# Linear attention with gapless context loads, and key sums from four GpSimd additions and one product

## The chip, the cores and the metric

The kernel is one launch on one core of a Trainium2 chip. The time is the device time of that launch in microseconds; the span of a profile is the time from the first to the last instruction of one profiled execution. Engines are named as in the profile: PE is TensorE (PEld its weight loads), DVE is VectorE, ACT is ScalarE, POOL is GpSimd, SP is SyncE, which here only issues DMAs.

## What is computed

Four attention layers follow each other on `x` (32 batch items of 56 tokens, 128 channels), each with the same context of 32 x 1500 x 128, all float32. Only the first layer is touched. For each item:

```python
Q_phi = elu(query)                      # 56 x 128
K_phi = elu(key)                        # 1500 x 128, key = value = context
KV = einsum('bnd,bne->bde', K_phi, value)
Z = 1.0 / (einsum('bnd,bd->bn', Q_phi, K_phi.sum(axis=1)) + 1e-6)
attn = einsum('bnd,bde->bne', Q_phi, KV) * Z[..., None]
x = query + attn                        # then a LayerNorm
```

`K_phi.sum(axis=1)` is the key sum: 128 numbers per item.

## The kernel before

`build` runs one stage after another, each in a block of its own that ends with all engines together. `load_phase` loads and transposes `x`; `linear_attention` is the stage of the change; then come the LayerNorms and projections, self attention, cross attention, full attention and the quantised layer. `linear_attention` also writes the transposed context of each item to DRAM (`ctx_turned`), which later stages read.

One item is a context matrix of 1500 rows. Row number 12 p + j lies on partition p (of KP = 125), slot j (of NJ = 12), so a partition holds 12 rows that are neighbours in DRAM, 6144 B. The tile `cn` has a 129th column in each slot that holds ones, set once per buffer by POOL (L264). There are four `cn` buffers. The loop over 32 items (`sweep`) writes out its first four steps, then loops, then drains. In step n the engines do:

- SP (L241 to L253) waits until item n-4 has been transposed, its product `kvp` is done (`kv_done`) and its `phi` is ready, and loads item n in two DMAs, of 112 and of 13 partitions (`CN_PARTS`). Each row of 128 floats is a piece of its own, because in the tile the next row begins 129 floats on. After the first four items SP issues 28 weight transfers (L257).
- DVE clips the item at zero (L311, `neg`), ACT takes the exponential (L354), and DVE makes `phi` = max(exp - 1, x) of the item before (L332).
- PE transposes the 12 slots of item n (L283), ACT copies them in three pieces to `ct` (L359, `turned_copied`), and POOL issues the store of `ct` to DRAM (L268).
- PE multiplies `phi` of item n-2 with `cn` of item n-2, all 129 columns, summed over the 12 slots (L292, `kvp`). Columns 0 to 127 are KV, column 128 is the key sum, thanks to the ones. DVE copies both to SBUF (L339, and L340, which spreads the sum over 128 columns).
- PE multiplies both with the queries of item n-3 (L300), ACT adds the epsilon (L350), DVE inverts and multiplies (L322, L324).

Each engine works strictly in its written order; semaphores named in the code join them. float32 products take two passes of weights and matmul each.

Of the kernel before, what the change touches and what calls it, by code (L numbers as in the profile page):

```python
# [5 lines left out]
ALU = mybir.AluOpType  # L6
# [6 lines left out]
B, NQ, NK, D = 32, 56, 1500, 128  # L13
# [204 lines left out]
def linear_attention(nc, m, w, ctx_in, ctx_turned):  # L218


    with ExitStack() as ctx:
        sb, ps, sem = memory(nc, ctx, "l0_")
        cn = [sb(f"cn{r}", [KP, NJ, D + 1]) for r in range(4)]
        neg = [sb(f"neg{p}", [KP, NJ, D]) for p in range(2)]
        phi = [sb(f"phi{p}", [KP, NJ, D]) for p in range(2)]
        ct = [sb(f"ct{p}", [128, NK]) for p in range(2)]
        kv = [sb(f"kv{p}", [128, 2, D]) for p in range(2)]
        den = [sb(f"den{p}", [128, NQ]) for p in range(2)]
# [4 lines left out]
        ctx_loaded = [sem(f"ctx_loaded{r}") for r in range(4)]  # L233
        ctx_stored = [sem(f"ctx_stored{p}") for p in range(2)]
        weights_loaded, loads = sem("weights_loaded"), weight_loads(m, w)[:EARLY]
        names = ("ones_set", "clipped", "exped", "phi_ready", "turned", "turned_copied",
                 "kv_done", "kv_copied", "ratio_done", "den_shifted", "den_inverted", "ratio_copied")
        (ones_set, clipped, exped, phi_ready, turned, turned_copied,
         kv_done, kv_copied, ratio_done, den_shifted, den_inverted, ratio_copied) = (sem(s) for s in names)

        with nc.Block() as block:  # L241
            @block.sync
            def _(sp):
                def step(n, r, live):
                    if live(4):
                        sp.wait_ge(turned, 3 * (n - 3))
                        sp.wait_ge(kv_done, n - 3)
                        sp.wait_ge(phi_ready, n - 3)
                    else:
                        sp.wait_ge(ones_set, 4)  # L250
                    rows = ctx_in[bass.ds(n, 1)].rearrange("o (p j) d -> (o p) j d", j=NJ)
                    for a, b in CN_PARTS:
                        sp.dma_start(cn[r][a:b, :, 0:D], rows[a:b]).then_inc(ctx_loaded[r], 16)  # L253

                def load_weights():
                    for dst, src in loads:
                        sp.dma_start(dst, src).then_inc(weights_loaded, 16)  # L257
                sweep(sp, step, 0, buffers=4, aside=load_weights)
                sp.wait_ge(weights_loaded, 16 * len(loads))

            @block.gpsimd
            def _(pool):
                for r in range(4):
                    pool.memset(cn[r][:, :, D:D + 1], 1.0).then_inc(ones_set, 1)  # L264

                def step(n, p, live):
                    pool.wait_ge(turned_copied, 3 * n + 3)
                    pool.dma_start(ctx_turned[bass.ds(n, 1)].rearrange("o d k -> (o d) k"), ct[p][:, :]  # L268
                                   ).then_inc(ctx_stored[p], 16)
                sweep(pool, step, 0)  # L270
                for p in range(2):
                    pool.wait_ge(ctx_stored[p], 16 * PAIRS)

            @block.tensor
            def _(pe):
                def step(n, r, live):
                    p = r % 2
                    if live(0):
                        pe.wait_ge(ctx_loaded[r], transfers(n, r, len(CN_PARTS), 4))
                        for j in range(NJ):  # L280
                            if j % 4 == 0 and live(1):
                                pe.wait_ge(turned_copied, 3 * n - 2 + j // 4)
                            last = pe.transpose(tp[:, j // 4, KP * (j % 4):KP * (j % 4) + KP], cn[r][:, j, 0:D],  # L283
                                                m.ident[0:KP, 0:KP])
                            if j % 4 == 3:
                                last.then_inc(turned, 1)
                    if live(2):
# [1 line left out]
                        if live(4):  # L289
                            pe.wait_ge(kv_copied, 2 * n - 6)  # L290
                        for j in range(NJ):
                            last = pe.matmul(kvp[:, p, 0:D + 1], phi[p][:, j, :], cn[(r - 2) % 4][:, j, :],  # L292
                                             start=j == 0, stop=j == NJ - 1)
                        last.then_inc(kv_done, 1)
                    if live(3):
                        pe.wait_ge(kv_copied, 2 * n - 4)
                        if live(4):
# [8 lines left out]
            def _(dve):  # L306
                def clip(n, r, live):
                    dve.wait_ge(ctx_loaded[r], transfers(n, r, len(CN_PARTS), 4))
                    if live(2):
                        dve.wait_ge(phi_ready, n - 1)  # L310
                    dve.tensor_scalar(neg[r % 2][:, :, :], cn[r][:, :, 0:D], 0.0, None, ALU.min  # L311
                                      ).then_inc(clipped, 1)

                def step(n, r, live):
# [11 lines left out]
                    if live(1):  # L326
                        q = (r - 1) % 4
                        dve.wait_ge(exped, n)
                        if live(3):
                            dve.wait_ge(kv_done, n - 2)  # L330

                        dve.scalar_tensor_tensor(out=phi[q % 2][:, :, :], in0=neg[q % 2][:, :, :], scalar=-1.0,  # L332
                                                 in1=cn[q][:, :, 0:D], op0=ALU.add, op1=ALU.max
                                                 ).then_inc(phi_ready, 1)
                    if live(2):
                        dve.wait_ge(kv_done, n - 1)
# [1604 lines left out]
```

## Time and profile before

| | |
|---|---|
| Median of 3 runs | 2575.98 us (2573.08 to 2579.17) |
| The profiled execution | 2577.91 us |
| Its span | 2576.4 us |
| PE busy | 2203.3 us (86%) |
| DVE busy | 1802.3 us (70%) |
| ACT busy | 1416.5 us (55%) |
| POOL busy | 708.9 us (28%) |
| HBM read, written | 127.01 MB, 25.49 MB |

The page also cuts the span into 40 slices of 64 us. The stage of the change lies in slices 1 to 4, where the DMA engines are busy for 7 to 9 tenths; they are idle in the slices after it. Shares over the whole span say little about one stage, so the stage is read by windows, waits and timelines of its own.

### The profile page before, as it was taken

To read this page: it belongs to the slowest core of one execution; us is meant where nothing else is said; L and a number is where in the kernel's file an instruction comes from. 1 tells how busy PE (TensorE), PEld (TensorE's weight loads), DVE (VectorE), ACT (ScalarE), POOL (GpSimd) and SP (SyncE) were. 2 spreads that over 40 slices of the span, in tenths; PEclk is the share of its full clock that TensorE was granted. 3 is DMA by queue.
4 is the path that set the end of the run, shared out by engine and by line. 5 is a ranking of instruction groups with operands and counts; after the bars stand their busy time and mean duration, and the time that the engine had idled before them with its cause. 6 is when DMAs were issued, how large, how long until landed. Compare 5 with 4: busy or idle time off the path is not lost. (4 is left out here: it accounts for less than half of the span.)

```text
span 2576.4 us, 60397 instructions
## 1 busy us (share of the span) xinstructions
PE 2203.3 (86%) x20341; PEld 1461.8 (57%) x20341; DVE 1802.3 (70%) x3608; ACT 1416.5 (55%) x2639; POOL 708.9 (28%) x538
## 2 busy tenths in 40 slices
PE   4777799869999999999987999544698888888888
PEld 4777477526666666666644767222365555555553
DVE  3555454567777777777734565799499999999984
ACT  2444232236666666666633444322398888888862
POOL 0000122111111111111000000232276666666640
PEclk7998655579999999999988999755699999999989
DMA  7896000013333223332206775000011111111100
GB/s 185 226 238 178 2 0 0 0 49 84 90 89 85 79 74 89 89 89 79 58 1 169 225 223 147 1 0 0 36 49 37 36 36 36 36 36 47 37 1 15
DMA packets 107834, 190.20 MB, mean 74 GB/s; under 512 B 19550, under 2 KB 74846, under 8 KB 107774
## 3 DMA queue, kind: packets, MB, share of 16 engines
q1 hardware_dynamic: 98558, 140.26, 19.8%
q0 software_dynamic: 9216, 49.16, 6.9%
q8 instruction: 36, 0.59, 0.1%
q14 instruction: 24, 0.20, 0.0%
HBM read 127.01 MB, written 25.49 MB: 59 GB/s over the span
## 5 line engine op out<-in xcount | busy, mean ns | idle before, releaser
L1025 DVE TENSOR_REDUCE c_part<-c_mxp 128x1 f32<-128x500 f32 x672 | 429.4, 674 | 172.7 <-PE c_mxp L914 168.4
L1634 ACT ACTIVATE c_e<-c_sp,alpha 128x750 f32<-128x750 f32 x448 | 392.8, 882 | 23.6 <-PE c_sp L1578 21.5
L998 ACT ACTIVATE c_e<-c_stp 125x896 f32<-125x896 f32 x384 | 351.9, 917 | 97.3 <-PE c_stp L926 96.8
L1592 PE MATMUL c_tp<-ident_h,c_ph 128*128 128x128 f16 x2688 | 230.6, 223 | 72.7 <-DVE c_pt L1654 70.8
L1592 PEld LDWEIGHTS c_tp<-ident_h,c_ph 128*128 128x128 f16 x2688 | 181.2, 100 | 167.6 <-DVE c_pt L1654 113.3
L914 PE MATMUL c_mxp<-c_kh,c_qb 128*128 128x500 f16 x672 | 254.4, 380 | 3.1 <-DVE c_part L1025 2.2
L1654 DVE TENSOR_SCALAR c_pt<-c_tp 125x768 bf16<-125x768 f16 x448 | 246.2, 550 | 3.4 <-PE c_tp L1592 1.9
L1548 POOL TENSOR_SCALAR c_ki<-c_clipped 128x500 bf16<-128x500 bf16 x96 | 191.8, 1998 | 151.6 <-DVE c_clipped L1665 139.5
L941 PE MATMUL c_pvp<-c_e,c_vx 125*32 125x168 f32 (+1 forms) x6144 | 226.9, 265 | 0.6 <-ACT c_e L998 0.4
L1698 DVE TENSOR_SCALAR c_ph<-c_e,c_inv 128x1500 f16<-128x1500 f32 x224 | 224.1, 1000 | 4.3
L941 PEld LDWEIGHTS c_pvp<-c_e,c_vx 125*32 125x32 f32 x6144 | 160.3, 109 | 117.1 <-issue 90.2
L868 POOL TENSOR_TENSOR c_qs<-qst,mask_quad_ 96x224 f16<-96x224 f32 (+1 forms) x128 | 67.5, 556 | 577.2 <-PE c_stp L926 577.2
L1578 PE MATMUL c_sp<-c_ki,c_qb 128*128 128x375 bf16 x896 | 224.2, 333 | 0.8 <-ACT c_e L1634 0.8
L926 PE MATMUL c_stp<-c_qs,c_ks 103*128 103x224 f16 x1536 | 210.8, 259 | 6.0 <-ACT c_e L998 2.3
L1548 POOL TENSOR_SCALAR c_vi<-c_clipped 125x512 bf16<-125x512 bf16 x96 | 196.2, 2044 | 60.4 <-DVE c_clipped L1665 59.1
L1643 ACT ACTIVATE c_rounded<-c_pp,round,rdelta 128x500 f32<-128x500 f32 (+1 forms) x192 | 148.4, 773 | 95.5 <-PE c_pp L1562 82.3
L926 PEld LDWEIGHTS c_stp<-c_qs,c_ks 103*128 103x128 f16 x1536 | 146.3, 98 | 81.2 <-issue 31.7
L1287 ACT ACTIVATE f_e<-f_sp,f_shift 56x500 f32<-56x500 f32 x96 | 63.4, 665 | 124.2 <-DVE f_shift L1320 124.2
L980 ACT ACTIVATE c_kh<-c_pp,bk 128x500 f16<-128x500 f32 x96 | 65.0, 677 | 112.5 <-PE c_pp L891 112.5
L891 PE MATMUL c_pp<-c_ct,wkv 128*128 128x500 f32 x192 | 109.4, 653 | 20.3 <-DVE c_ks L1006 14.9
L1562 PE MATMUL c_pp<-c_ct,a2wk 128*128 128x500 f32 x192 | 114.3, 680 | 8.5 <-DMA c_ct<-ctx_turned 6.7
L283 PE MATMUL l_tp<-ident_,l_cn 125*128 125x125 f32 x384 | 58.3, 312 | 70.3 <-DMA l_cn<-in_ctx 70.3
(262 smaller groups left out, 4057.2 us busy)
## 6 DMA issues: line engine op xcount, KB each, us to landing
c_ct<-ctx_turned SPq DMA_DIRECT2D x64, 750.0 KB
ctx_turned<-l_ct POOLq DMA_DIRECT2D x32, 750.0 KB, 4.7
c_ks<-c_kh SPq DMA_DIRECT2D x256, 93.8 KB
f_ct<-ctx_turned SPq DMA_DIRECT2D x32, 750.0 KB, 4.3
f_cn<-in_ctx POOLq DMA_DIRECT2D x32, 750.0 KB
l_cn<-in_ctx SPq DMA_DIRECT2D x32, 672.0 KB
c_ks<-c_kl SPq DMA_DIRECT2D x128, 93.8 KB
l_cn<-in_ctx SPq DMA_DIRECT2D x32, 78.0 KB
```

The costliest lines, as they stand in the source:

```text
L914: pe.matmul(mxp[:, (PIECES * p + s) % 2, 0:500], qh[p][:, 128 * (s // 3):128 * (s // 3) + 128], kh[p][:, 500 * (s % 3):500 * (s % 3) + 500 ...
L926: last = pe.matmul(stp[:, 2 * (j % 2) + g // 2, 224 * (g % 2):224 * (g % 2) + 224], ks[p][:, g, KP * j:KP * j + 128], qs[p][:, 224 * g:224 ...
L941: last = pe.matmul(pvp[q:q + 32, c:c + width], vx[p][:, j, g, :], e[:, j % 4, NQ * h:NQ * h + width], start=(j == 0 and g < 4), stop=j == ...
L998: act.activation(e[:, j % 4, :].rearrange("p (a c) -> p a c", a=2), stp[0:KP, 2 * (j % 2):2 * (j % 2) + 2, 0:448], ACT.Exp, scale=SCALE).t ...
L1025: dve.reduce_max(part[:, s // 3, s % 3:s % 3 + 1], mxp[:, (PIECES * p + s) % 2, 0:500], axis=AX.X).then_inc(piece_max, 1)
L1548: pool.tensor_scalar(out, clipped[t % 2][0:rows, 0:width], -128.0, None, ALU.max).then_inc(proj_ready, 1)
L1578: last = pe.matmul(sp_[:, 2 * h + k, 0:375], qb[p][:, 128 * t:128 * t + 128], ki[p][:, HALF * h + 375 * k:HALF * h + 375 * k + 375], start ...
L1592: last = pe.transpose(tp[:, h, 128 * k:128 * k + 128], ph[r][:, KP * j:KP * j + 128], m.ident_h[:, :])
L1634: act.activation(e[r][:, HALF * h:HALF * h + HALF].rearrange("p (k c) -> p k c", k=2), sp_[:, 2 * h:2 * h + 2, 0:375], ACT.Exp, scale=m.al ...
L1643: act.activation(rounded[t % 2][0:rows, 0:width], pp[0:rows, 0:width], ACT.Identity, bias=m.round[0:rows, 0:1], scale=m.rdelta[0:rows, d:d ...
L1654: dve.tensor_scalar(pt[p][:, 6 * h:6 * h + 6, 128 * t:128 * t + 128], tp[0:KP, h, 0:6 * 128].rearrange("p (j c) -> p j c", j=6), HALF_ROUN ...
L1698: dve.tensor_scalar(ph[r][:, 0:NK], e[r][:, :], inv[:, 0:1], HALF_ROUND, ALU.mult, ALU.add).then_inc(p_ready, 1)
```

## The change

The tile `cn` loses its 129th column, so that the 12 rows of a partition are gapless in DRAM and in SBUF, 6144 B in one run. The memsets of that column and SP's wait for them go. The key sum is made otherwise: POOL adds `phi` over its 12 slots, 12 to 6 (`half`), 6 to 3 (`quarter`), and then two additions of one slot (`pair_sum`, `phis`), each with a wait for the one before. They stand behind the store of the next item in POOL's order. PE multiplies `phis` with one column of ones as a last product into column 128 of `kvp`; it waits for `phis_ready` before that, and `kv_done` is signalled by this product. DVE's `phi` waits in addition for the first POOL addition of the item whose buffer it overwrites. The diff, without the lines that only rename `cn[..][:, :, 0:D]` to `cn[..][:, :, :]` and extend lists of semaphores:

```diff
-        cn = [sb(f"cn{r}", [KP, NJ, D + 1]) for r in range(4)]
+        cn = [sb(f"cn{r}", [KP, NJ, D]) for r in range(4)]
+        half = sb("half", [KP, NJ // 2, D])
+        quarter = sb("quarter", [KP, NJ // 4, D])
+        pair_sum = sb("pair_sum", [KP, D])
+        phis = [sb(f"phis{p}", [KP, D]) for p in range(2)]
+        ones = sb("ones", [KP, 1])
...
-                    else:
-                        sp.wait_ge(ones_set, 4)
...
-                        sp.dma_start(cn[r][a:b, :, 0:D], rows[a:b]).then_inc(ctx_loaded[r], 16)
+                        sp.dma_start(cn[r][a:b, :, :], rows[a:b]).then_inc(ctx_loaded[r], 16)
...
-                for r in range(4):
-                    pool.memset(cn[r][:, :, D:D + 1], 1.0).then_inc(ones_set, 1)
+                pool.memset(ones[:, :], 1.0).then_inc(ones_set, 1)
+
+                def add_keys(a, p, live):
+                    if live(2):
+                        pool.wait_ge(quartered, a)
+                    pool.wait_ge(phi_ready, a + 1)
+                    pool.tensor_tensor(half[:, :, :], phi[p][:, 0:6, :], phi[p][:, 6:12, :], ALU.add
+                                       ).then_inc(halved, 1)
+                    if live(2):
+                        pool.wait_ge(phis_ready, a)
+                    pool.wait_ge(halved, a + 1)
+                    pool.tensor_tensor(quarter[:, :, :], half[:, 0:3, :], half[:, 3:6, :], ALU.add
+                                       ).then_inc(quartered, 1)
+                    pool.wait_ge(quartered, a + 1)
+                    pool.tensor_tensor(pair_sum[:, :], quarter[:, 0, :], quarter[:, 1, :], ALU.add
+                                       ).then_inc(paired, 1)
+                    if live(3):
+                        pool.wait_ge(kv_done, a - 1)
+                    pool.wait_ge(paired, a + 1)
+                    pool.tensor_tensor(phis[p][:, :], pair_sum[:, :], quarter[:, 2, :], ALU.add
+                                       ).then_inc(phis_ready, 1)
 
                 def step(n, p, live):
-                    pool.wait_ge(turned_copied, 3 * n + 3)
-                    pool.dma_start(ctx_turned[bass.ds(n, 1)].rearrange("o d k -> (o d) k"), ct[p][:, :]
-                                   ).then_inc(ctx_stored[p], 16)
-                sweep(pool, step, 0)
+                    if live(0):
+                        pool.wait_ge(turned_copied, 3 * n + 3)
+                        pool.dma_start(ctx_turned[bass.ds(n, 1)].rearrange("o d k -> (o d) k"), ct[p][:, :]
+                                       ).then_inc(ctx_stored[p], 16)
+                    if live(1):
+                        add_keys(n - 1, 1 - p, live)
+                sweep(pool, step, 1)
...
             def _(pe):
+                pe.wait_ge(ones_set, 1)
...
                         for j in range(NJ):
-                            last = pe.matmul(kvp[:, p, 0:D + 1], phi[p][:, j, :], cn[(r - 2) % 4][:, j, :],
-                                             start=j == 0, stop=j == NJ - 1)
-                        last.then_inc(kv_done, 1)
+                            pe.matmul(kvp[:, p, 0:D], phi[p][:, j, :], cn[(r - 2) % 4][:, j, :],
+                                      start=j == 0, stop=j == NJ - 1)
+                        pe.wait_ge(phis_ready, n - 1)
+                        pe.matmul(kvp[:, p, D:D + 1], phis[p][:, :], ones[:, :], start=True, stop=True
+                                  ).then_inc(kv_done, 1)
...
                         dve.wait_ge(exped, n)
                         if live(3):
+                            dve.wait_ge(halved, n - 2)
                             dve.wait_ge(kv_done, n - 2)
```

## Rows read from the trace of the kernel before

**Rows 1.** Busy time by stretch: length, each engine, PEclk, DMA share, GB/s.
```profile
20.00:60.00 40.00, 18.80 (x110) 17.90 (x111) 11.59 (x15) 13.11 (x18) 2.44 (x4) 0.63 1.07 255
60.00:235.00 175.00, 132.05 (x1055) 129.16 (x1054) 99.66 (x157) 85.56 (x134) 13.81 (x26) 0.92 0.87 228
```

**Rows 2.** Waits, 60 to 235 us: engine, for whom; total, times, longest.
```profile
PE l_tp L283 <- DMA l_cn<-in_ctx: 42.9, 22, 2.8
...
SPq L248 <- PE l_kvp L292: 112.6, 26, 9.1
```

**Rows 3.** Timeline, 127 to 144 us: start, length, engine, operation [idle before].
```profile
128.02 1.52 ACT L359 ACTIVATE l_ct<-l_tp 128x500 f32<-128x500 f32 x3
...
130.13 14.88 SPq L253 DMA_DIRECT2D l_cn<-in_ctx  x6
130.20 0.53 POOL L268 DMA_DIRECT2D ctx_turned<-l_ct  x1 [5.59 <-ACT l_ct L359]
...
133.97 2.85 PE L292 MATMUL l_kvp<-l_cn,l_phi 125*128 125x129 f32 x24
...
138.54 0.96 DVE L311 TENSOR_SCALAR l_neg<-l_cn 125x1536 f32<-125x1536 f32 x1 [1.20 <-DMA l_cn<-in_ctx]
...
138.56 1.49 PE L283 MATMUL l_tp<-ident_,l_cn 125*128 125x125 f32 x12 [1.35 <-DMA l_cn<-in_ctx]
...
139.89 2.85 PE L292 MATMUL l_kvp<-l_cn,l_phi 125*128 125x129 f32 x24
...
142.95 2.06 SPq L253 DMA_DIRECT2D l_cn<-in_ctx  x2
```

**Rows 4.** Timeline of DVE, 236 to 238 us: the clip of the last item.
```profile
237.39 0.96 DVE L311 TENSOR_SCALAR l_neg<-l_cn 125x1536 f32<-125x1536 f32 x1 [0.25 <-DMA l_cn<-in_ctx]
```

**Rows 5.** DMA queues, 60 to 235 us: packets, MB, share of 16 engines.
```profile
q1 hardware_dynamic: 39546, 19.87, 49.7%
q0 software_dynamic: 3744, 19.97, 37.3%
```

**Rows 6.** DMA queues, 1500 to 1600 us, full attention: q0 loads context rows gapless.
```profile
q0 software_dynamic: 1872, 9.98, 41.9%
```

**Rows 7.** DMA queue of SP, 1800 to 1850 us: two loads of 128 partitions.
```profile
q1 hardware_dynamic: 288, 1.54, 8.3%
```

**Rows 8.** Issues on SP by line: count, ns least/median/most, first and last start.
```profile
L253 SPq DMA_DIRECT2D l_cn<-in_ctx x52: 606/747/1999, 65.0 to 229.6; - x52
...
L826 SPq DMA_DIRECT2D c_ct<-ctx_turned x32: 327/336/427, 538.8 to 1240.4; - x32
```

**Rows 9.** Timeline of the start, SP's issues and DVE's clip of item 4.
```profile
19.70 12.12 SPq L253 DMA_DIRECT2D l_cn<-in_ctx  x8
...
50.45 5.19 SPq L253 DMA_DIRECT2D l_cn<-in_ctx  x4
...
57.97 0.96 DVE L311 TENSOR_SCALAR l_neg<-l_cn 125x1536 f32<-125x1536 f32 x1 [12.65 <-DMA l_cn<-in_ctx]
```

**Rows 10.** Groups of POOL over the span: shapes, count | busy us, mean ns.
```profile
L1548 POOL TENSOR_SCALAR c_ki<-c_clipped 128x500 bf16<-128x500 bf16 x96 | 191.8, 1998 | 151.6 <-DVE c_clipped L1665 139.5 <-PE c_sp L1578 12.1
...
L525 POOL TENSOR_TENSOR s_qb<-q_,mask_head_ 128x896 f32<-128x896 f32 x32 | 53.9, 1687 | 180.0 <-PE s_sp L540 128.4 <-SPq L518 51.6
```

**Rows 11.** Timeline, 2058.5 to 2060 us, and line L1684 in 2000 to 2100.
```profile
2058.98 1.68 POOL L1532 TENSOR_TENSOR c_qb<-qi,mask_head_ 128x896 bf16<-128x896 f32 x1
2059.03 1.65 DVE L1684 SCALAR_TENSOR_TENSOR c_total<-c_half,delta 128x1 f32<-128x1 f32 x1
...
L1684 DVE SCALAR_TENSOR_TENSOR c_total<-c_half,delta x35: 210/219/1648, 2001.3 to 2099.0; 128x1 f32<-128x1 f32 x35
```

**Rows 12.** Timeline of PE at 1501.7 us: a product of one column, two passes.
```profile
1501.73 0.26 PE L1239 MATMUL f_bkp<-l2bk,f_ql 128*56 128x1 f32 x2
```

**Rows 13.** Timeline, 243 to 248 us: the last `phi` and the last `kvp`.
```profile
243.11 1.75 DVE L332 SCALAR_TENSOR_TENSOR l_phi<-l_neg,l_cn 125x1536 f32<-125x1536 f32 x1
...
245.03 2.91 PE L292 MATMUL l_kvp<-l_cn,l_phi 125*128 125x129 f32 x24
```

More of the change, by code:

```diff
@@ L235, in linear_attention @@
         weights_loaded, loads = sem("weights_loaded"), weight_loads(m, w)[:EARLY]
-        names = ("ones_set", "clipped", "exped", "phi_ready", "turned", "turned_copied",
+        names = ("ones_set", "phis_ready", "halved", "quartered", "paired", "clipped", "exped", "phi_ready", "turned", "turned_copied",
                  "kv_done", "kv_copied", "ratio_done", "den_shifted", "den_inverted", "ratio_copied")
-        (ones_set, clipped, exped, phi_ready, turned, turned_copied,
+        (ones_set, phis_ready, halved, quartered, paired, clipped, exped, phi_ready, turned, turned_copied,
          kv_done, kv_copied, ratio_done, den_shifted, den_inverted, ratio_copied) = (sem(s) for s in names)
@@ L282, in step @@
                                 pe.wait_ge(turned_copied, 3 * n - 2 + j // 4)
-                            last = pe.transpose(tp[:, j // 4, KP * (j % 4):KP * (j % 4) + KP], cn[r][:, j, 0:D],
+                            last = pe.transpose(tp[:, j // 4, KP * (j % 4):KP * (j % 4) + KP], cn[r][:, j, :],
                                                 m.ident[0:KP, 0:KP])
@@ L310, in clip @@
                         dve.wait_ge(phi_ready, n - 1)
-                    dve.tensor_scalar(neg[r % 2][:, :, :], cn[r][:, :, 0:D], 0.0, None, ALU.min
+                    dve.tensor_scalar(neg[r % 2][:, :, :], cn[r][:, :, :], 0.0, None, ALU.min
                                       ).then_inc(clipped, 1)
@@ L329, in step @@
                         if live(3):
+                            dve.wait_ge(halved, n - 2)
                             dve.wait_ge(kv_done, n - 2)
                         dve.scalar_tensor_tensor(out=phi[q % 2][:, :, :], in0=neg[q % 2][:, :, :], scalar=-1.0,
-                                                 in1=cn[q][:, :, 0:D], op0=ALU.add, op1=ALU.max
+                                                 in1=cn[q][:, :, :], op0=ALU.add, op1=ALU.max
                                                  ).then_inc(phi_ready, 1)
```

## The prediction

> **What bounds the kernel now.** The change touches one stage, `linear_attention`, which runs from about 19.7 to 251 us of the span. All stages stand in blocks of their own, and the next one begins only when this one has ended, so whatever the stage gains or loses is gained or lost whole, and nothing behind it should move. I therefore read only this stretch. The table by stretch [rows 1] has three parts: a start (20 to 60 us, DMA share 1.07, half of it at the low clock), a steady part (60 to 235 us: PE busy 132 of 175 us, DVE 100, ACT 86, POOL 14, DMA share 0.87) and a short tail. No engine is full. The waits of the steady part [rows 2] show PE idle 42.9 us in 22 waits for the load of `cn`, and the loads themselves held back by SP's wait for the product `kvp`; POOL sleeps 5.59 us between a store and the next [rows 3].
>
> So it is a loop, and the timeline of one turn shows it [rows 3]. SP issues the load for item n+2 when PE has finished `kvp` of step n. One such load is issued at 130.13 and releases DVE at 138.54 and PE at 138.56: 8.43 us. PE then works from 138.56 to 142.74 (12 transposes, 24 passes for `kvp`), and 0.21 us later, at 142.95, SP issues the load after the next. 8.43 + 4.18 + 0.21 = 12.82 us for two steps, 6.41 each. Over the whole steady part the clip L311 starts at 57.97 for item 4 [rows 9] and at 237.39 for item 31 [rows 4]: 179.42 us for 27 steps, 6.645 each (some turns at the low clock included). **A step costs half of (load latency + PE time + issue).** Shortening the load by 1 us gives 0.5 us a step; lengthening PE's way to `kv_done` by 0.25 us costs 0.125.
>
> **The change part by part.**
>
> *Gapless loads.* The DMA's work per load comes from the queue rows [rows 5]: q1 held 49.7% of 175 us for 19.87 MB, 25.9 loads of 0.768 MB, so 3.36 us a load; a store on q0 takes 37.3% x 175 / 26 = 2.51 us. How long the gapless form takes isn't shown on this queue with these rows; there are two neighbours. `full_attention` loads the same rows gapless into 125 partitions through POOL's queue [rows 6]: 41.9% of 100 us for 9.98 MB, 3.22 us a load. The cross stages load 128 partitions of 6000 B through SP's queue [rows 7]: 8.3% of 50 us for two, 2.08 us a load. The first has the partitions, the second the queue; 112 + 13 partitions is neither, so I take the middle, 2.65 us: 0.7 us less. Bounds: 0.1 and 1.3 us less. Then SP's own work: an issue with 12 pieces per partition takes 747 ns in the median, up to 1999, while one of 128 pieces takes 336 [rows 8]. Load latency includes the writing out of the pieces before the engines have full work; two issues take 2.06 us where 0.67 would do. I take 0.5 us of that as latency saved (bounds 0 and 1.0; most of it runs beside the moving of the first pieces). Together the load lands 1.2 us sooner: bounds 0.1 and 2.3 us.
>
> The Trainium skill, DMA: Bandwidth & Descriptors, section Specifications, speaks against this change: it gives 512 B or more as the transfer size for line rate, and 512 B is what the loads have now. By that rule the pieces would cost nothing and only the issue time could shrink. The row for 125 gapless partitions sides with it, the one for 128 doesn't; it is the first rival below.
>
> *The column of ones goes, one product comes.* `kvp` streams 128 columns for 129, worth 24 x 1 column, nothing to be seen. The new product has one column; a one-column pair of passes takes 0.26 us [rows 12]. It lies between the last `kvp` pass and `kv_done`, on the loop: +0.25 us on PE's 4.18. Bounds 0.15 and 0.4. Behind PE's new wait for `phis_ready` stand the numerator and denominator products and the next transposes, and DVE's copies and SP's next load wait for `kv_done`, so a late sum delays all.
>
> *Four additions on POOL.* 768 + 384 + 128 + 128 = 1408 elements a partition. POOL's f32 `tensor_tensor` took 1687 ns for 896 [rows 10], 1.88 ns each: 2.65 us, and some 0.3 us for waits between them, 2.95. POOL's step: ct copied at 128.02 + 1.52 = 129.54, store issued 130.20, 0.53 long [rows 3], so 1.19 us, and 2.95 behind it: 4.1 us of a step of over 6. The sum for the item before is ready 4.1 us after the third `ct` copy (129.54), and PE wants it at the end of the next step's `kvp`, 136.82 in today's time, 7.3 us after. It is hidden with 3.2 us to spare, 2.7 if steps shorten by half a microsecond. Stores stand behind the additions on POOL, but POOL is done before the next `ct`.
>
> *Where POOL and DVE meet.* In the quantised stage a DVE operation of 0.22 us on two SBUF operands took 1.65 us; it began 0.05 us after a two-operand POOL operation of 1.68 us and ended with it [rows 11]. So a two-operand DVE operation waits for a running POOL one. The Trainium skill, SBUF — State Buffer, section "SBUF: two separate sides", calls this an exclusive lock that the loser waits out in full, in both directions; the row agrees for DVE as the loser. Here `phi` (L332, 1.76 us, two operands) may wait 1.45 us for the first addition, or the additions may wait for it and the clip (0.96 us). Worst case both ways: POOL 4.1 + 1.76 + 0.96 = 6.8 us. But `phi` has the rest of its own step and the next step's transposes before its product needs it, and DVE idles 1.20 us before a clip besides [rows 3], so I cost it at nothing, with +0.2 us a step as the bound. DVE's new wait for `halved` looks two items back: nothing.
>
> *The start.* SP no longer waits for four memsets: a few tenths at most, not counted. The first eight issues took 12.12 us, then come 28 weight transfers, and only at 50.45 is the load of item 4 issued; it lands at 57.97, DVE having idled 12.65 us [rows 9]. With issues of 0.34 us SP would reach that load some 9.4 us sooner. But the DMA engines are full all the while (share 1.07 [rows 1]), and their work shrinks by only five loads of 0.7 us, 3.5 us. I take 6 us, bounds 3 and 10.
>
> *The tail.* The last `phi` ends at 243.11 + 1.75 = 244.86 and the last `kvp` runs from 245.03 to 247.94 [rows 13]. POOL sums the last item in 2.95 us from 244.9 at best, or from about 245.5 since the one before comes first: 248.4, and PE adds 0.25. The end moves by 0.5 to 1 us, the two products before it add 0.5: +1.5 us, bounds 0.5 and 3.
>
> *Sum.* Step: (-1.2 + 0.25) / 2 = -0.475 us, times 27 = -12.8 us. Start -6, tail +1.5: -17.3 us. The profiled execution took 2577.9 us (span 2576.4 and 1.5 around it), 1.9 above the median of 2576.0 of the three runs. 2577.9 - 17.3 = 2560.6, and against the median 2558.7; I say **2559**. Bounds: load 0.1 sooner, product 0.4, lock 0.2: step +0.15 + 0.2 = +0.35, x 27 = +9.5, start -3, tail +3: 2585. Load 2.3 sooner, product 0.15: -1.07 x 27 = -29, start -10, tail 0.5: 2537.
>
> **The rivals.**
>
> A. *The pieces were never the price.* A load's time is set by how 125 partitions fall on the engines, as the 3.22 us of the gapless neighbour say, and the issue runs beside the transfer. Step (-0.15 + 0.25) / 2 = +0.05, x 27 = +1.4; start -4; tail +1.5: -1, **2575**. For it: rows 6 against rows 5, 4% apart. Against it: that neighbour goes through the other queue. Chance 0.20.
>
> B. *Everything comes.* The load behaves as the 128-partition row: 1.3 + 0.7 us sooner. (-2.0 + 0.25) / 2 x 27 = -23.6, start -9, tail +1.5: -31, **2545**. PE needs 4.7 us and POOL 4.1, so the step of 5.8 has room. Fewer waits of PE may also hold the high clock: now it is 0.92 in the mean [rows 1]. Against it: 128 divides evenly, 112 + 13 does not. Chance 0.15.
>
> C. *POOL becomes the bound: slower.* POOL's plain one-operand operation on 500 elements took 2.0 us [rows 10], 4 ns each. If additions run at that rate, or pay it through the lock, they take 1408 x 4 = 5.6 us; with store and waits 7.1 us, and with one wait for a DVE operation 7.4. `phis_ready` then sets the loop at 7.4: +0.75 x 27 = +20; start -5, tail +4: +19, **2595**. It decides from additions of about 5 us in all (5 + 1.2 = 6.2, my own step). For it: the lock row, and a span of 2.7 us of DVE work a step that can collide. Against: the `tensor_tensor` row, the same operation on f32, says 1.9 ns. Chance 0.12.
>
> D. *The load isn't what it says:* still pieces of 512 B, or a slower split of the 13 partitions. Then only the product and the tail are left: 0.125 x 27 + 1.5 = +5, **2581**. `full_attention` shows that the same view gives whole rows: 0.03.
>
> **How the numbers follow.** My forecast has 0.50 (its own range 2548 to 2570). About 0.2% (5 us) is what a measurement can tell from no change. Faster by more: 0.48 of my forecast's 0.50, B's 0.15 and 0.05 of A: 0.68. Within: 0.15 of A and the 0.02 left of the forecast: 0.17. Slower by more: C and D: 0.15. The range for 8 in 10 takes in B's 2545 and most of A: 2542 to 2580; C is left out.
>
> **What the profile would show.** Two `l_cn` issues near 0.34 us each; q1's packets some 12 times fewer in the stage, its work per load near 2.65 us; the issue of a load to DVE's release near 7.2 us; L311 every 6.2 us; item 4 near 52 us; POOL additions 1.45, 0.75, 0.3 and 0.3 us; no wait of PE for POOL. Wrong would make me: `kv_done` waiting on `phis`; a store now sharing time evenly with a load in pieces as large as its own and pushing the landing back; the clock falling more often.

## The result, and the profile after

The changed kernel takes **2591.55 us** (median of 6 runs, 2588.26 to 2594.75), the kernel before 2573.27 us in the same sessions (median of 6). The ratio is **1.0068 (95% interval 1.0058 to 1.0078)**: 0.7% slower, where 2559 was forecast. The profiled execution took 2588.36 us, its span 2586.8. Of the recorded times rival C's 2595 is the nearest, 3.5 us off; whether C's reasons came true as well is told further down.

What changed lies in the stage. Its last `ratio` ends at 251.4 us before and at 265.8 after, 14.4 us later. Behind it nothing was changed, and there the time differs from execution to execution: from the stage's end to the end of the span are 2325.0 us before, 2321.0 after, and 2319.0 to 2327.9 over all fourteen profiles here. So the medians differ by 18.3 us and the two profiled spans by 10.4, and a gain or loss of a few microseconds is better read in the stage. The 14.4 us split in three, read at the clip (DVE's `l_neg<-l_cn`), L311 before and L340 after:

| | before | after | difference | forecast |
|---|---|---|---|---|
| clip of item 4 starts | 57.97 [rows 9] | 54.14 | -3.8 | -6 |
| 27 steps to the clip of item 31, each | 6.645 [rows 4] | 7.07 | +0.425, x 27 = +11.5 | -12.8 |
| from there to the last `ratio` | 13.97 | 20.73 | +6.8 | +1.5 |
| sum | | | +14.4 | -17.3 |

First the table by stretch of the changed kernel (length, then PE, PEld, DVE, ACT, POOL busy, clock, DMA share, GB/s), which answers to rows 1.

```profile
20.00:60.00 40.00, 23.39 (x144) 22.03 (x144) 13.05 (x15) 14.96 (x21) 16.07 (x18) 0.70 0.90 258
60.00:235.00 175.00, 140.86 (x1049) 135.82 (x1048) 135.04 (x150) 79.01 (x122) 154.72 (x123) 0.89 0.67 215
```

In the steady part POOL goes from 13.81 busy us to 154.72 of 175, and DVE from 99.66 to 135.04 although it has no more to compute: its clips take longer (2.64 us in the mean against 0.96), while `phi` takes 1.76 us in both. The DMA share falls from 0.87 to 0.67, and the granted clock from 0.92 to 0.89; what the clock has to do with the loss was not separated. Its waits for the same stretch (engine, for whom; total, times, longest), which answer to rows 2:

```profile
ACT l_neg L384 <- DVE l_neg L340: 55.7, 25, 2.6
...
DVE l_kv L369 <- PE l_kvp L322: 36.7, 25, 2.4
PE l_kvp L322 <- POOL l_phis L285: 33.4, 21, 2.3
POOL ctx_turned L291 <- issue: 10.8, 24, 0.6
```

PE's 42.9 us of waiting for the load [rows 2] is gone. In its place PE waits 33.4 us for the last of POOL's additions, and POOL waits for nobody: "issue" is all that is left of its idle time. The loads come in time. Their queues in the same stretch (packets, MB, share), and the issue of the loads on SP, beside rows 5 and 8:

```profile
q1 hardware_dynamic: 3818, 19.10, 37.8%
q0 software_dynamic: 3472, 18.53, 28.6%
```

```profile
L256 SPq DMA_DIRECT2D l_cn<-in_ctx x64: 317/318/971, 19.5 to 238.3; - x64
```

37.8% x 175 / (19.10 / 0.768) = 2.66 us of work a load, with a tenth of the packets, and 318 ns an issue: both as the prediction had them (2.65, 0.34). What it had wrong most is POOL. The groups of POOL and the clip on DVE, 60 to 235 us (shape, count | busy us, mean ns | idle before):

```profile
L340 DVE TENSOR_SCALAR l_neg<-l_cn 125x1536 f32<-125x1536 f32 x25 | 65.9, 2636 | 1.0 <-DMA l_cn<-in_ctx 0.3 <-issue 0.2
L280 POOL TENSOR_TENSOR l_pair_sum<-l_quarter 125x128 f32<-125x128 f32 x25 | 46.5, 1861 | 2.0
L272 POOL TENSOR_TENSOR l_half<-l_phi 125x768 f32<-125x768 f32 x25 | 45.7, 1827 | 0.6
L277 POOL TENSOR_TENSOR l_quarter<-l_half 125x384 f32<-125x384 f32 x25 | 38.6, 1545 | 3.6
L285 POOL TENSOR_TENSOR l_phis<-l_pair_sum,l_quarter 125x128 f32<-125x128 f32 x24 | 12.2, 509 | 3.4
```

1.83 + 1.55 + 1.86 + 0.51 = **5.74 us a step** for the additions, where 2.65 was forecast (2.95 with 0.3 us of waits between them). The two small ones have the same shape, and one takes 1.86 us, the other 0.51. The clip, 0.96 us before, takes 2.64. One step of the timeline (start, length) shows why:

```profile
130.21 0.57 POOL L291 DMA_DIRECT2D ctx_turned<-l_ct  x1 [0.56 <-issue]
...
130.53 2.93 DVE L340 TENSOR_SCALAR l_neg<-l_cn 125x1536 f32<-125x1536 f32 x1
...
130.81 1.82 POOL L272 TENSOR_TENSOR l_half<-l_phi 125x768 f32<-125x768 f32 x1
...
132.78 1.54 POOL L277 TENSOR_TENSOR l_quarter<-l_half 125x384 f32<-125x384 f32 x1
...
134.22 1.76 DVE L362 SCALAR_TENSOR_TENSOR l_phi<-l_neg,l_cn 125x1536 f32<-125x1536 f32 x1
134.40 1.89 POOL L280 TENSOR_TENSOR l_pair_sum<-l_quarter 125x128 f32<-125x128 f32 x1
...
136.43 0.45 POOL L285 TENSOR_TENSOR l_phis<-l_pair_sum,l_quarter 125x128 f32<-125x128 f32 x1
...
136.94 0.38 PE L322 MATMUL l_kvp<-l_ones,l_phis 125*128 125x1 f32 x2 [2.31 <-POOL l_phis L285]
137.22 0.57 POOL L291 DMA_DIRECT2D ctx_turned<-l_ct  x1 [0.33 <-issue]
```

The clip and the first addition run at the same time, and the clip ends 0.83 us after that addition has ended, a little less than its own 0.96. `quarter` begins while the clip still runs and ends 0.86 us after it. `pair_sum` begins 0.18 us after `phi` and ends 0.31 us after it. So each of the two engines sits waiting while the other's operation runs. This recurs: from item 5 to item 31 every clip ends 0.82 to 0.84 us after its `half`, whether the clip's record begins before that of `half` (16 of 27 steps, by up to 0.34 us) or after it. POOL's chain from one store to the next is 0.57 + 5.70 + 0.74 of gaps = 7.01 us, and the step is 7.07. PE, whose new product hangs on that chain, holds back `kv_done`, and with it DVE's copies and the next load.

The price without company is in the same trace. At the start of the stage DVE idles 7.49 us ahead of the clip of item 4, and the four additions of an earlier item fall into that gap, but for the first 0.4 us:

```profile
46.22 1.81 POOL L272 TENSOR_TENSOR l_half<-l_phi 125x768 f32<-125x768 f32 x1
48.18 0.99 POOL L277 TENSOR_TENSOR l_quarter<-l_half 125x384 f32<-125x384 f32 x1
49.25 0.45 POOL L280 TENSOR_TENSOR l_pair_sum<-l_quarter 125x128 f32<-125x128 f32 x1
49.85 0.45 POOL L285 TENSOR_TENSOR l_phis<-l_pair_sum,l_quarter 125x128 f32<-125x128 f32 x1
...
54.14 0.96 DVE L340 TENSOR_SCALAR l_neg<-l_cn 125x1536 f32<-125x1536 f32 x1 [7.49 <-DMA l_cn<-in_ctx]
```

1.81 + 0.99 + 0.45 + 0.45 = 3.70 us (the last item's, in the drain of the stage, are the same: 1.81, 1.00, 0.46, 0.45). So of the 3.09 us by which the additions passed the forecast (5.74 against 2.65), 1.05 are their own price (3.70 against 2.65), and 2.04 are the meeting with DVE (5.74 against 3.70).

### The profile page after: what moved, and what is told of

Its sections match the earlier page's. It is cut to its first block and busy times, and to the rows that moved or that the text cites. A ratio compares the mean times of both kernels' runs of the same rounds, so it can differ in the third digit from the quotient of the medians.

```text
span 2586.8 us, 60778 instructions
## 1 busy us (share of the span) xinstructions
PE 2220.6 (86%) x20405; PEld 1478.3 (57%) x20405; DVE 1847.9 (71%) x3608; ACT 1417.2 (55%) x2639; POOL 887.2 (34%) x663
## 3 DMA queue, kind: packets, MB, share of 16 engines
q1 hardware_dynamic: 54558, 140.26, 18.7%
## 5 line engine op out<-in xcount | busy, mean ns | idle before, releaser
L1684 DVE TENSOR_SCALAR c_pt<-c_tp 125x768 bf16<-125x768 f16 x448 | 246.2, 550 | 3.4 <-PE c_tp L1622 2.1
L1256 POOL DMA_DIRECT2D f_cn<-in_ctx x32 | 16.8, 526 | 295.0 <-PE f_op L1282 199.9
```

The source lines that it names most:

```text
L1684: dve.tensor_scalar(pt[p][:, 6 * h:6 * h + 6, 128 * t:128 * t + 128], tp[0:KP, h, 0:6 * 128].rearrange("p (j c) -> p j c", j=6), HALF_ROUN ...
```

## The experiments

**Theory:** the gapless loads gain what was forecast, and POOL's additions, lengthened by DVE, take it back and more. **Rival 1:** the loads gained nothing or hurt. **Rival 2:** the additions' own length is enough, DVE has no part in it. A step is measured from the clip of item 4 to that of item 31, divided by 27. All ratios are to the kernel before; expectations of step and time are from before each run. The code shows the main lines of an edit, with "..." where something is cut; the semaphore waits that go with it are left out.

### The additions left out

```
-   if live(1):
-       add_keys(n - 1, 1 - p, live)
...
-   pe.wait_ge(phis_ready, n - 1)
-   pe.matmul(kvp[:, p, D:D+1], phis[p][:, :], ones[:, :], ...)
+   pe.matmul(kvp[:, p, D:D+1], phi[p][:, 0, :], ones[:, :], ...)
```

> The changed kernel without the four POOL additions: the last product takes slot 0 of phi in place of the sum over the slots (the key sum is left out, so the time is that of the gapless loads and the extra product alone). Theory (POOL's chain of store issue, additions and waits for DVE sets the step at 7.07 us): no PE wait for POOL is left, the load loop rules again, steps near 6.2 us, q1 work per load 2.66 us, item 4 near 54 us, about 2561 us. Rival 1 (the gapless loads themselves or their sharing with the store cost the time and the wait for POOL is a by-product): steps above 6.65, 2573 us or more. Rival 2 (gapless pieces are worth nothing): steps 6.65 to 6.75, about 2571 us from the start alone.

Measured: 2563.31 us, ratio 0.995 (0.9935 to 0.9965); step **6.215**, stage end 237.1. Its waits and its queue of loads, 60 to 235 us:

```profile
POOL ctx_turned L271 <- ACT l_ct L365: 153.4, 27, 7.3
...
PE l_tp L288 <- DMA l_cn<-in_ctx: 31.2, 21, 3.2
```

```profile
q1 hardware_dynamic: 4004, 19.97, 46.5%
```

PE waits for loads again, and POOL has 153 us of idle time. This is the prediction's step (6.17) without its additions. The additions cost 7.07 - 6.215 = 0.855 us a step, 23 us in all, and the rest of their 28 us in the tail. One thing came out smaller than in the sum: from `kv_done` (DVE's first copy of `kv`) to the clip that the load releases takes 8.54 us in the mean before and 7.84 here (items 9 to 31). The load lands 0.7 us sooner, not 1.2. Its work in the queue is also larger than in the changed kernel: 46.5% x 175 / 26 = 3.13 us a load, 0.23 less than before and not 0.7; the stores, on the other side, land after 7.8 us in the median where before took 4.7.

### The additions alone, on the old loads

```
-   cn = [sb(f"cn{r}", [KP, NJ, D]) for r in range(4)]
+   cn = [sb(f"cn{r}", [KP, NJ, D + 1]) for r in range(4)]
...
-   sp.dma_start(cn[r][a:b, :, :], rows[a:b])
+   sp.dma_start(cn[r][a:b, :, 0:D], rows[a:b])
```

> The additions and the product, but cn keeps its 129-float pitch, so the loads go in pieces of 512 B as before. Theory: the step is POOL's, 7.0 to 7.1 us as in the changed kernel; only the start is some 4 us later: 2595 us. Rival 1 (the gapless loads cost the time): near the kernel before, 2575 us. Rival 2: 2592 to 2600.

Measured: 2596.77 us, 1.0083 (1.0069 to 1.0097); step **7.085**, the same as after. With loads of 512 B pieces PE waits 18.7 us for `phis` and 15.4 for the load; the two nearly balance, and the step is that of POOL. Rival 1 falls: the loss is there without the gapless loads, so they have no part in it. Behind POOL their gain isn't seen in the step either, only at the start (item 4 at 58.24 here, 54.14 after).

### The clip moved from DVE to ACT

```
-   dve.tensor_scalar(neg[...], cn[r][...], 0.0, None, ALU.min)
...
+   act.activation(neg[p][...], cn[r][...], ACT.Relu, scale=-1.0)
-   act.activation(neg[p][...], neg[p][...], ACT.Exp)
+   act.activation(neg[p][...], neg[p][...], ACT.Exp, scale=-1.0)
```

> The changed kernel with the clip moved from DVE to ACT (relu of -x, then exp of minus that; same result). POOL does exactly the same additions. Theory with the exclusive port: the clip no longer collides, the second addition falls from 1.55 to 1.0 us, the third still waits for phi (1.87), the step falls by 0.55 us to 6.5, 2576 us. Rival (POOL's additions are simply that long, DVE has no part in it): additions 1.8, 1.5, 1.9, 0.45 as now, step 7.07, 2591 us. Against both: ACT gets 1.5 us a step more, 4.8 of 6.5.

Measured: 2572.66 us, 0.9991 (0.9982 to 1.0); step **6.48**. POOL's groups and `phi`:

```profile
L277 POOL TENSOR_TENSOR l_quarter<-l_half 125x384 f32<-125x384 f32 x27 | 63.2, 2342 | 3.9
L353 DVE SCALAR_TENSOR_TENSOR l_phi<-l_neg,l_cn 125x1536 f32<-125x1536 f32 x27 | 60.7, 2249 | 0.0
L272 POOL TENSOR_TENSOR l_half<-l_phi 125x768 f32<-125x768 f32 x28 | 51.4, 1837 | 0.6
...
L280 POOL TENSOR_TENSOR l_pair_sum<-l_quarter 125x128 f32<-125x128 f32 x27 | 12.2, 453 | 2.1
L285 POOL TENSOR_TENSOR l_phis<-l_pair_sum,l_quarter 125x128 f32<-125x128 f32 x27 | 12.2, 453 | 3.9
```

The additions have not been touched, and they shrink from 5.74 to 5.09 us because DVE has one large operation fewer; the step shrinks with them. Rival 2 falls: the additions' length depends on what DVE does. The expectation had the remaining meeting in the wrong place. It is now `quarter` that waits for `phi` (2.34 us where 0.99 is its own length), `phi` is longer as well (2.25 us against 1.76), and `pair_sum` is at its 0.45. Who meets whom follows from the order in time, and moves when anything else is moved.

### Half of the keys

```
-   pool.tensor_tensor(half[...], phi[p][:, 0:6, :], phi[p][:, 6:12, :], ALU.add)
...
-   pool.tensor_tensor(quarter[...], half[:, 0:3, :], half[:, 3:6, :], ALU.add)
+   pool.tensor_tensor(quarter[...], phi[p][:, 0:3, :], phi[p][:, 3:6, :], ALU.add)
```

> The first addition is left out and the second reads slots 0 to 5 of phi, so half of the key sum is left out; the third and fourth stay. Theory: POOL's step is 0.4 + 0.6 + 1.55 + 1.9 + 0.45 and 0.3 of waits = 5.2 us, below the load loop; steps as with no additions, 6.2 us, and only the tail is longer by 2 us: 2563 us. If the step still stays near 7, POOL's length isn't the bound but its place: then 2585 or more.

Measured: 2556.66 us, 0.9932 (0.9913 to 0.9951); step **6.127**. The three groups of additions, 60 to 235 us:

```profile
L274 POOL TENSOR_TENSOR l_quarter<-l_phi 125x384 f32<-125x384 f32 x29 | 29.2, 1007 | 0.7
L277 POOL TENSOR_TENSOR l_pair_sum<-l_quarter 125x128 f32<-125x128 f32 x29 | 28.4, 978 | 2.3
L282 POOL TENSOR_TENSOR l_phis<-l_pair_sum,l_quarter 125x128 f32<-125x128 f32 x29 | 18.9, 650 | 4.2
```

They take 1.01 + 0.98 + 0.65 = 2.64 us with their waits for DVE, what the forecast had for all four, and the step comes out near its 6.17. PE waits 22.8 us for loads and 4.2 for `phis`. So additions of this total length on POOL, in this place, are nearly hidden; it is their length that costs, own and added. The median is near the forecast's 2559 too, but 6.7 us below that of the run without additions, of which only 1.2 lie in the stage (its end is 235.9 against 237.1); the rest is in code that neither run changes.

### The key sum on DVE, alone and with the clip on ACT

```
-   add_keys(n - 1, 1 - p, live)          # POOL
...
+   dve.tensor_reduce(phis[q % 2][:, :], phi[q % 2][...].rearrange("p j d -> p d j"),
+                     AX.X, ALU.add)
```

> Gapless loads, and the key sum as one reduction over the 12 slots on DVE instead of four additions on POOL; POOL only issues stores. The reduction reads 1536 elements with a stride; at the rate of phi it takes some 1.7 us. Theory (it is POOL's chain and its collisions that cost, the loads gain): DVE's step is 0.96 + 0.5 + 0.22 + 1.76 + 1.7 + 0.57 and gaps = 5.9 us, just under the load loop; step 6.2 to 6.4 us, 2562 to 2567 us. Rival (a sum of 1536 elements is too dear anywhere): the step is DVE's, 6.7 or more, 2575 us.

Measured: 2570.99 us, 0.9993 (0.9983 to 1.0002); step **6.616**. The expectation was missed: one reduction over the 12 keys takes 2.82 us, not 1.7.

```profile
L343 DVE TENSOR_REDUCE l_phis<-l_phi 125x128 f32<-125x1536 f32 x27 | 76.0, 2817 | 0.9
...
L318 DVE TENSOR_SCALAR l_neg<-l_cn 125x1536 f32<-125x1536 f32 x27 | 25.6, 949 | 0.0
```

DVE is busy 164.85 us of 170 (60 to 230 us) and sets the step. With POOL out of the way the clip is back at 0.95 us on unchanged code. With the clip on ACT as well:

> As the kernel before this one in the list, and the clip is on ACT. DVE's step falls to 4.9 us, ACT's is 4.8. If the load loop then rules alone, the step is that of the kernel with no additions, 6.2 us, 2560 us; if it is lower than 6.1 the clip's place between load and transposes mattered; above 6.4 ACT's longer chain (relu, exp, then the three copies that free the transposes' banks) has become the loop, 2570 us.

Measured: 2558.64 us, 0.9946 (0.9932 to 0.996); step **5.94**. This computes all of the reference, and is 0.5% faster than the kernel before. It is below the 6.2 of the run without additions, so the 6.2 is no floor of the loads. By the expectation the clip's place between load and transposes then mattered; no run tests that by itself. What a step costs without the load's latency is told under eight buffers.

### The first addition on DVE, three on POOL

```
-   pool.tensor_tensor(half[...], phi[p][:, 0:6, :], phi[p][:, 6:12, :], ALU.add)
...
+   dve.tensor_tensor(half[...], phi[q % 2][:, 0:6, :], phi[q % 2][:, 6:12, :], ALU.add)
```

> The first addition (768 elements) on DVE, the other three on POOL. Theory: POOL's step is 0.5 + 0.6 + 1.0 to 2.4 + 0.45 + 0.45 + 0.3 = 3.3 to 4.7 us, DVE's 5.0 + 0.9 = 5.9 at most plus one wait behind a POOL addition; the load loop rules: step 6.2 us, 2562 us. Rival (any addition on POOL in the loop costs): 6.6 or more, 2575 us.

Measured: 2558.83 us, 0.9948 (0.9931 to 0.9966); step **6.03**. `half` takes 0.96 us on DVE (1.82 on POOL), POOL's three take 1.01 + 1.06 + 0.49 = 2.56 us, and the clip 1.95. The rival (6.6 or more for any addition on POOL) falls. It computes all of the reference too, and is the smallest edit to the changed kernel here that turns the loss into a gain: the chain on POOL gets shorter by one addition, and that one costs DVE half as much.

### Eight buffers for the context

The prediction says that half of the load's latency is in each step because a load waits for the step before last. Eight buffers take that wait away. The same edit went into five kernels:

```
-   cn = [sb(f"cn{r}", ...) for r in range(4)]
+   cn = [sb(f"cn{r}", ...) for r in range(8)]
...
-   if live(4):
-       sp.wait_ge(kv_done, n - 3)
+   if live(8):
+       sp.wait_ge(kv_done, n - 7)
```

In the changed kernel:

> The changed kernel with eight cn buffers instead of four and nothing else. Theory (POOL's chain of 7.0 us sets the step): no gain in the steady part, steps stay at 7.0 to 7.1 us; item 4 lands as before; 2590 us. Rival (the load loop, lengthened by the later kv_done, sets the step): with loads issued six steps ahead it falls to 6.2 or less, 2567 us.

Measured: 2594.30 us, 1.0077 (1.0062 to 1.0091); step **7.067** against 7.07. The load's latency is worth nothing once POOL sets the step. Its waits:

```profile
PEld l_kvp L323 <- POOL l_phis L286: 39.5, 21, 3.0
...
PE l_kvp L323 <- POOL l_phis L286: 35.5, 21, 2.8
```

In the kernel before:

> The kernel before (gapped loads, column of ones) with eight cn buffers. Theory of the load loop: latency is hidden, what remains is DMA work of 3.36 + 2.51 = 5.9 us a step and PE's 4.6; step 5.9 to 6.1, 2557 us. If it falls well below 5.9 to 5.0, the shares of the queues overstate the work (packets of the two queues overlapping) and the pieces of 512 B are no bound either: 2535 us. Rival (throughput already sets 6.65): 2573 us.

Measured: **2538.93 us, 0.9859 (0.9843 to 0.9876)**; step **5.20**, stage end 213.7. The step is far below the 5.9 to 6.1 expected of it. Of the kernels that compute all of the reference it is the fastest here, ahead of both kernels of this case. Its waits, 60 to 235 us, and its queues between 120 and 190 us:

```profile
ACT l_ct L360 <- DMA ctx_turned<-l_ct: 33.5, 21, 3.8
...
PE l_tp L284 <- DMA l_cn<-in_ctx: 14.4, 1, 14.4
```

```profile
q1 hardware_dynamic: 21063, 10.58, 70.6%
q0 software_dynamic: 1987, 10.58, 39.2%
```

PE waits once for a load. 512 B pieces do not hold the kernel at 6.6 us a step; the wait for their latency did. The shares of the queues add up to 110%, so a share is time in which packets were under way, not a measure of throughput used up: the 3.36 us a load read from rows 5 are not a floor. What ACT waits for now is the store of two items ago (33.5 us).

The same with gapless loads and no additions:

> Gapless loads, no POOL additions (the product takes slot 0 of phi, the key sum is left out), eight cn buffers: what gapless loads are worth once latency is hidden, beside the kernel before with eight buffers (step 5.20 us, 2539 us). Theory (only latency counted, and the extra product is 0.25 us of PE): step 5.1 to 5.3 in the steady part, no better than gapped; with the earlier start of 4 us, 2535 to 2540 us. Rival (the load pieces still cost in the deep version): step 4.8 or less, 2528 us.

Measured: 2525.84 us, 0.9807 (0.9793 to 0.9822); step **4.89**, stage end 200.6: below the 5.1 to 5.3 expected, and nearer to the rival's 4.8. ACT again waits for the store, 27.0 us. Against the kernel before with eight buffers the gapless loads are worth 5.20 - 4.89 = 0.31 us a step and 5.5 us at the start, 13 us in all. That is an answer to rival A: the gapless form of the load (longer pieces and a shorter issue together) is worth something even where its latency is hidden, but less than the 0.6 us a step (half of 1.2) of the forecast.

Last, two ways to have gapless loads, eight buffers and the key sum, both with the clip on ACT. The reduction on DVE:

> The key sum on DVE, the clip on ACT and eight cn buffers, so that a load may be issued six steps ahead and no longer waits for the step two before. Theory (half the load latency is in every step): the loop is gone and the step falls to what the engines and queues need: DMA work 2.66 + 2.07 = 4.7 us, PE 4.7, DVE 4.9, ACT 4.8 plus waits, so 5.2 to 5.6 us, 27 x 0.8 = 22 us less, 2540 us. Rival (the transfers' throughput, not their latency, sets the step): it stays at 6.1 to 6.2, 2560 us.

Measured: 2550.47 us, 0.9915 (0.9902 to 0.9929); step **5.72**, with DVE busy 161.58 us of 170 (60 to 230 us). The step expected was 5.2 to 5.6. And the first addition on DVE, three on POOL:

> Gapless loads, eight buffers, clip on ACT, the first addition on DVE and the other three on POOL. DVE's step 0.5 + 0.22 + 1.76 + 0.96 + 0.56 and gaps = 4.3 us, ACT 4.8 to 5.1, PE 4.9, POOL 1.1 + 1.0 + 0.45 + 0.45 plus at most 1.8 of waits for DVE = 4.9. Step 5.2 to 5.4 us, against 5.72 with the reduction on DVE and eight buffers: 2539 to 2544 us. If the shared port costs more than one wait a step, 5.7 again, 2551 us.

Measured: 2550.74 us, 0.9916 (0.9899 to 0.9933); step **5.80**, where 5.2 to 5.4 was expected and 5.7 if the meeting cost more. Three groups of it, 60 to 235 us:

```profile
L348 DVE SCALAR_TENSOR_TENSOR l_phi<-l_neg,l_cn 125x1536 f32<-125x1536 f32 x28 | 61.2, 2186 | 0.0
L281 POOL TENSOR_TENSOR l_phis<-l_pair_sum,l_quarter 125x128 f32<-125x128 f32 x29 | 42.4, 1461 | 4.2
...
L276 POOL TENSOR_TENSOR l_pair_sum<-l_quarter 125x128 f32<-125x128 f32 x29 | 28.7, 989 | 2.3
```

`phis`, 0.45 us by itself, takes 1.46. Each of the two key sums, with the clip on ACT, costs 0.8 to 0.9 us a step against 4.89, which is more than the 0.31 that the gapless loads bring; in the first, DVE is nearly full, and in the second the three additions and `phi` still meet. The column of ones, which gets the sum from a pass that PE makes anyway, is the cheaper way by 12 us (2550.47 against 2538.93).

## Why the prediction was wrong, step by step

**What bounds the kernel** was right as far as it went: the loop of load latency and PE time is there, and taking the latency out of it gave 35 us (2574.4 to 2538.9 in the same sessions, ratio 0.9859, eight buffers). The loop was used only to price a shorter load, not to ask what it would be worth not to wait for one.

**Gapless loads, 1.2 us sooner:** 2.66 us of work and 318 ns an issue were met in the changed kernel, but with the step as short as forecast (the run without additions) the work is 3.13 us, close to the 3.22 of the gapless neighbour [rows 6]; the middle between two neighbours was luck where it held. The landing did not hold: 0.7 us sooner with the additions away. That the step came out as forecast all the same, 6.215 against 6.17, is luck in part. Half of 0.7 is 0.35; the other 0.08 of the 0.43 us is PE's part of the turn (2 x 6.645 - 8.54 = 4.75 us before, 2 x 6.215 - 7.84 = 4.59), which was forecast to grow by 0.25. It includes stretches at the lower clock: the granted clock of 60 to 235 us is 0.92 before and 0.96 in the run without additions, and a pass of `kvp` takes 290 ns in the mean before and 280 there. How much of the rest is the clock was not settled.

**The product, +0.25:** 0.38 us in the rows of after, 0.28 in the run without additions: within its bounds (0.15 to 0.4).

**Four additions on POOL, 2.65 us and 0.3 between them: the first term that failed.** They take 3.70 us alone; the gaps between them, 0.37 us in the step shown above, were about right. The row taken for the price [rows 10], 1.88 ns an element, is called "the same operation on f32", but it is one long multiplication by a mask, with broadcast operands. The three lengths of after, 0.45, 0.99 and 1.81 us for 128, 384 and 768 elements, lie on a line of 2.1 ns an element and 0.18 us an instruction, so four short additions carry 0.7 us that a rate per element does not show. The Trainium skill, GPSIMD Engine Reference, section "Elementwise — side-by-side cycle accounting", gives 4497 ns for an f32 addition of 2048 elements, 2.2 ns each; the rows agree with it, and an estimate from it (1408 x 2.2 = 3.1 us) would have been nearer than the row of another operation.

**Where POOL and DVE meet, "I cost it at nothing": the step that failed.** It was asked who could afford to be late, and `phi` could. That POOL's additions may wait as well was said, and then dropped from the sum; that the clip itself waits was not thought of. Both recur in every step: 2.04 us on POOL and 1.68 on the clip. The worst case of the text, "4.1 + 1.76 + 0.96 = 6.8 us" for POOL, is near the measured 7.01, partly by luck: it had the additions 1.05 us too short and the waits 0.7 too long. It was already above the forecast's own step of 6.2; a bound of +0.2 us could not stand beside it. Without the meeting the chain would have been 0.57 + 3.70 + 0.74 = 5.0 us, and with the meeting but the additions at their forecast length 0.57 + 2.65 + 2.04 + 0.74 = 6.0, both hidden (worked out, not run): it takes the meeting with DVE on top of the longer additions to cross the line, and the meeting is the larger part. The row read for the rule [rows 11] had DVE with two operands. The clip has one, and it waits too: 0.96 to 2.64 us. By the Trainium skill, SBUF — State Buffer, section "SBUF: two separate sides", a DVE operation in a two-port mode takes the lock as well as one with two SBUF inputs, and whichever comes second is blocked in full. The 2.64 us of the clip and the 1.86 of `pair_sum` agree with a wait in full, in both directions. By the starts in the records the order does not agree: in 16 of 27 steps the clip's record begins before that of `half`, and the clip is still the one that waits. That the clip runs in a two-port mode is nothing that a row shows; a row shows only that it takes 0.96 us for the 1536 elements a partition for which `phi` takes 1.76. The prediction had taken the lock from that page, but let only an operation with two operands wait on DVE's side.

**The start, -6:** -3.8 us, within its bounds. SP issues the first eight in 3.32 us instead of 12.12 and reaches the load of item 4 at 43.36 instead of 50.45, 7.1 us sooner; it lands only 3.8 sooner. What holds it back in between was not tested; the DMA engines are busy for 0.90 of this stretch.

**The tail, +1.5: wrong by 5.3 us.** In the drain the additions are the path with nothing beside them. The last rows of it:

```profile
253.71 2.07 DVE L362 SCALAR_TENSOR_TENSOR l_phi<-l_neg,l_cn 125x1536 f32<-125x1536 f32 x1
...
261.34 0.45 POOL L285 TENSOR_TENSOR l_phis<-l_pair_sum,l_quarter 125x128 f32<-125x128 f32 x1
...
261.85 0.38 PE L322 MATMUL l_kvp<-l_ones,l_phis 125*128 125x1 f32 x2 [0.42 <-POOL l_phis L285]
...
265.54 0.22 DVE L353 TENSOR_TENSOR ratio<-l_ndp,l_inv 128x56 f32<-128x56 f32 x1
```

From the end of the last `phi` (255.78) to the end of the last sum (261.79) are 6.0 us where 3.5 were counted: the sum of the item before is still under way, with a `quarter` of 2.34 us that waits for that `phi`, and then come the last four. Another 3.3 us fall ahead of that: the last `phi` ends 7.5 us after the last clip begins before, and 10.8 after, the clip itself being 2.0 us longer.

**The rivals.** C said that the loop turns on POOL when the additions reach "about 5 us in all", "or pay it through the lock"; they took 5.74, and 2595 was its time. Its mechanism holds in part. It came to 5.6 us by 4 ns an element, where the rows give 2.1 and the rest is waiting; its step of 7.4 was 0.3 too long, and its tail of +4 was 2.8 too short. That these cancel in part is luck. Its chance of 0.12 was too low: the argument against it was one row of another operation, run while DVE was not looked at. That row spoke of the rate and not of the meeting. The sum itself missed by the two terms above: the step that was to shrink by 0.475 us grew by 0.425. The range left C out and so ended at 2580. A and B turned on the loads, and the change by itself does not decide them, since its step no longer waits for loads; the run without additions does, and its step sides with the forecast (6.215, where A had 6.7 and B 5.8), while the landing, 0.7 us sooner, lies between A's 0.15 and the forecast's 1.2. D falls with the packets, a tenth of before. One reading was off and changed nothing: the start was called "half of it at the low clock", but the granted clock of its four quarters is 0.50, 0.52, 0.99 and 0.50.

## What to carry to other kernels

Work given to an idle engine is hidden only if the engine's whole chain, with the waits that it meets and causes, is shorter than the step that it should hide in; here POOL's additions and DVE's clip were both longer beside each other (5.74 us against 3.70, 2.64 against 0.96), so add the DVE operations of a step to its worst case and believe that sum until a run says otherwise. Where a loop pays a load's latency, first ask for more buffers: here they brought 35 us, and the faster load with its new sum brought a loss. A sum that comes as one more column of a product that PE makes anyway was not beaten here by either of two sums with instructions of their own.

## What the runs showed of the hardware

- A clip with one SBUF operand on DVE takes 0.96 us alone and 2.64 in the mean beside POOL's additions (0.95 to 2.99). POOL's addition of 128 elements takes 0.45 us alone and 1.86 beside `phi`; that of 384 takes 0.99, 1.55 or 2.34. ACT's clip of the same tile stays at 1.48 us beside both.
- f32 additions on POOL, 128 to 768 elements a partition: 0.18 us plus 2.1 ns an element. The addition of 768 elements takes 0.96 us on DVE.
- A reduction on DVE that reads 1536 elements with a stride and writes 128 takes 2.82 us, where the two-operand `phi` over the same 1536 takes 1.76.
- A store from POOL's queue landed after 4.7 us in the median before, 6.4 in the changed kernel and 7.8 with gapless loads and no additions. Neither part of the change delays it by itself: it is 4.7 with the additions on the old loads, and 3.8 with gapless loads and the reduction on DVE. What sets it was not found.
- The shares of two DMA queues added to 110% at 303 GB/s, so a queue's share cannot be read as throughput used up.
- Left open: how much of a gapless load's gain is the length of a row and how much the shorter issue; and whether some other way to the key sum fits under the 4.89 us that gapless loads and eight buffers allow. Neither was tried.
